# Gated delta-rule attention: scores' mask moved into the decay factors, and four buffers of attention factors

## The reference

```python
def step(S, xs):
    qt, kt, vt, gt, bt = xs
    S = S * jnp.exp(gt)[..., None, None]
    kv = jnp.einsum('bhk,bhkv->bhv', kt, S)
    delta = (vt - kv) * bt[..., None]
    S = S + jnp.einsum('bhk,bhv->bhkv', kt, delta)
    o = jnp.einsum('bhk,bhkv->bhv', qt * scale, S)
    return (S, o)
...
s = _L0_attn_ref(xn, ...)
g = _silu(_L0_ffn_ref(xn, ...))
x = x + s * g
```

## Time and profile before

| what | value |
|---|---|
| device time, median of 3 runs | 4069.94 us (4063.95 to 4076.19) |
| span of the profiled execution | 4068.1 us (its own device time is not given apart from the span) |
| PE busy | 3999.3 us, 98% |
| PEld busy | 3042.7 us, 75% |
| DVE busy | 3147.1 us, 77% |
| ACT busy | 2279.5 us, 56% |
| POOL busy | 1482.6 us, 36% |
| mean granted TensorE clock | 0.995 of full speed |

### The profile page before, as it was taken

How to read it: one execution, slowest core, us unless ns; L and a number is a source line. 1 busy time by engine, 2 the same in 40 slices (tenths; PEclk the granted TensorE clock), 3 DMA queues, 4 the chain that set the end, 5 groups by cost and what they waited for, 6 DMA issues and landing times. The chain is left out here.

```text
span 4068.1 us, 83861 instructions
## 1 busy us (share of the span) xinstructions
PE 3999.3 (98%) x29432; PEld 3042.7 (75%) x29432; DVE 3147.1 (77%) x6660; ACT 2279.5 (56%) x5904; POOL 1482.6 (36%) x1744
## 2 busy tenths in 40 slices
PE   7999999999999999999999999999999999999998
PEld 6788787787777777777777777777777777777775
DVE  6766666665588878888888887788888888877885
ACT  2222222222277676666767666766666676666664
POOL 2322232322133334333333333334444444444445
PEclk9999999999999999999999999999999999999999
DMA  5212111110534344434434454444444444454443
GB/s 151 51 34 49 31 43 49 25 49 21 163 94 105 105 110 103 104 101 102 102 97 108 105 144 128 110 129 120 111 119 116 114 125 125 119 131 125 119 107 97
DMA packets 813539, 400.89 MB, mean 99 GB/s; under 512 B 475584, under 2 KB 738752, under 8 KB 813120
## 3 DMA queue, kind: packets, MB, share of 16 engines
q1 hardware_dynamic: 777024, 340.30, 32.1%
q10 hardware_dynamic: 36096, 55.24, 4.9%
HBM read 242.70 MB, written 152.63 MB: 97 GB/s over the span
## 5 line engine op out<-in xcount | busy, mean ns | idle before, releaser
L1239 PE MATMUL bank<-xtile,wt 128*128 128x259 f32 x4096 | 1073.2, 391 | 5.2 <-PEq L764 2.5
L1239 PEld LDWEIGHTS bank<-xtile,wt 128*128 128x128 f32 x4096 | 736.9, 191 | 148.7 <-issue 59.6
L1631 ACT ACTIVATE xyinv<-bank 128x512 f16<-128x512 f32 x768 | 451.7, 590 | 320.2 <-PE bank L1574 317.2
L1888 PE MATMUL bank<-wot,xnt 128*128 128x512 f32 x1024 | 537.6, 611 | 1.1 <-DVE xnt L1847 0.8
L1243 PE MATMUL bank<-wt,xtile 128*128 128x512 f32 x1024 | 521.1, 607 | 0.0
L1607 DVE TENSOR_TENSOR wlev<-bank,mask 128x256 f16<-128x256 f32 x768 | 316.8, 413 | 149.9 <-PE bank L1574 146.1
L548 PE MATMUL bank<-hb,wt 128*128 128x128 f32 x2816 | 376.4, 277 | 8.4 <-DVE part L588 5.7
L1269 DVE SCALAR_TENSOR_TENSOR vraw<-bank,taps,vraw 128x256 f32<-128x256 f32 x768 | 363.3, 476 | 27.3 <-ACT vraw L1262 13.5
L548 PEld LDWEIGHTS bank<-hb,wt 128*128 128x128 f32 x2816 | 350.2, 194 | 17.5 <-issue 7.2
L611 POOL TENSOR_TENSOR hid<-part 128x256 f32<-128x256 f32 x176 | 139.0, 790 | 474.2 <-ACT part L603 474.2
L1574 PEld LDWEIGHTS bank<-xyinv,lth 128*128 128x128 f16 x3584 | 202.1, 98 | 146.2 <-issue 71.6
(11 more groups left out here) (217 smaller groups left out, 8609.8 us busy)
## 6 DMA issues: line engine op xcount, KB each, us to landing
v_scratch<-vraw SPq DMA_DIRECT2D x64, 512.0 KB, 3.3
vtok<-v_scratch SPq DMA_DIRECT2D x512, 64.0 KB, 2.2
x_scratch<-tq SPq DMA_DIRECT2D x508, 64.0 KB, 1.8
xnt<-x_scratch SPq DMA_DIRECT2D x508, 64.0 KB, 2.5
grows<-row_scratch ACTq DMA_DIRECT2D x126, 256.0 KB, 3.7
k_scratch<-kraw SPq DMA_DIRECT2D x32, 512.0 KB, 2.6
ktok<-k_scratch SPq DMA_DIRECT2D x256, 64.0 KB, 2.5
b_scratch<-kraw SPq DMA_DIRECT2D x256, 64.0 KB, 1.8
```

The costliest lines, as they stand in the source:

```text
L1239: j = pe.matmul(b_p[:, 0:WIN], wt[:, k, c:c + P], xtile[:, par, k, :], **st)
L1631: act.activation(dst, b_inv[p][:].rearrange("p (a h b s) -> p a h b s", a=2, h=HEADS, s=z), ACT.Copy).then_inc(s[f"xy_sb{p}"], 1)
L1888: i = pe.matmul(b_o[:], xnt[:, h], wot[:, h], start=(h == 0), stop=(h == GV - 1))
```

## The change

The multiplication with the masks is gone as a step. The scan now starts from -300, its mask is 1 everywhere but on the diagonal, and the first element of every row of decays is -300. So the running sum left of the diagonal is at most -300, its exponential is 0, and `gam` itself is masked. `dve_lower` and `dve_attend` read the scores where they lie, in PSUM. The factor 64 enters as a logarithm in the bias, so both products carry it, and `act_eps` multiplies by 1/64 in exchange. What `dve_lower` leaves on the diagonal is overwritten with 64 by GpSimd's `affine_select`, in place of the subtraction of a mask. The bank of the scores is free when `lower` and `attend` are both done. `pt` has four buffers in place of three. `SP` waits once for the -300 to be written before it stores the first rows. The planner's tables follow: no `scores` on VectorE, `decay` 1.25 in place of 1.22, `unit` 0.67 in place of 1.16.

```diff
-PIPE = 3
+PIPE = 4
+FAR = 300.0
...
-M_LT, M_LE, M_OFF, M_NEG, M_L0T, M_EVEN = range(6)
-M_PAST = M_EVEN + (LEVELS - 1) // 2
-N_MASK = M_PAST + HEADS
+M_L0T, M_EVEN = range(2)
+M_OFF = M_EVEN + (LEVELS - 1) // 2
+N_MASK = M_OFF + HEADS
...
-    m[:, M_OFF] = 1.0 - np.eye(P)
-    m[:, M_NEG] = -SCALED * np.eye(P)
+    m[:, M_OFF:] = (1.0 - np.eye(P))[:, None, :]
...
-    m[:, M_LT] = SCALED * (r[:, None] < r[None, :])
-    m[:, M_LE] = r[:, None] <= r[None, :]
-    m[:, M_PAST:] = (r[:, None] < r[None, :])[:, None, :]
...
-                link(dve.tensor_scalar(gout[:, u % 2, :, :, G_LNB, :], soft[:, 1].rearrange("p j (g h) -> p j g h", g=GROUPS), -1.0, None, ALU.mult))
+                link(dve.tensor_scalar(gout[:, u % 2, :, :, G_LNB, :], soft[:, 1].rearrange("p j (g h) -> p j g h", g=GROUPS), -1.0, math.log(SCALED), ALU.mult, ALU.add))
...
-            act.activation(grow[:, u % 2], bank[0][0:w, 3 * w:3 * w + P], ACT.Copy).then_inc(s["gc_exp"], 1)
+            act.activation(grow[:, u % 2, 1:P], bank[0][0:w, 3 * w + 1:3 * w + P], ACT.Copy).then_inc(s["gc_exp"], 1)
...
+                    if u == 0:
+                        sp.wait_ge(s["set"], 3)
...
+                pool.memset(grow[:, :, 0:1], -FAR).then_inc(s["set"], 1)
...
-                return [(s["kq_sb"], q + 1)]
+                return [(s["lt_sb"], q + 1), (s["pt_sb"], q + 1)]
...
-        def dve_scores(dve, n):
-            dve.wait_ge(s["kq_ps"], n + 1)
-            if n:
-                dve.wait_ge(s["lt_sb"], n)
-                dve.wait_ge(s["pt_sb"], n)
-            dve.tensor_tensor(kqm[:].rearrange("p (t h) c -> p t h c", t=2), tile_bank("scores", n)[:].rearrange("p (t h c) -> p t h c", t=2, h=KPB),
-                              mask[:, M_LT:M_LE + 1, :].unsqueeze(2).broadcast_to([P, 2, KPB, P]), ALU.mult).then_inc(s["kq_sb"], 1)
...
-            dve.tensor_tensor_scan(gam[:].rearrange("p h c -> p (h c)"), grows[:, n % 2], mask[:, M_PAST:, :].rearrange("p h c -> p (h c)"), 0.0, ALU.add, ALU.mult).then_inc(s["sum_sb"], 1)
+            dve.tensor_tensor_scan(gam[:].rearrange("p h c -> p (h c)"), grows[:, n % 2], mask[:, M_OFF:, :].rearrange("p h c -> p (h c)"), -FAR, ALU.add, ALU.mult).then_inc(s["sum_sb"], 1)
...
-        scored = lambda lo: kqm[:, lo:lo + KPB].unsqueeze(2).broadcast_to([P, KPB, REP, P])
+        scored = lambda n, t: tile_bank("scores", n)[:].rearrange("p (t h c) -> p t h c", t=2, h=KPB)[:, t].unsqueeze(2).broadcast_to([P, KPB, REP, P])
...
-            dve.wait_ge(s["kq_sb"], n + 1)
+            dve.wait_ge(s["kq_ps"], n + 1)
...
-            dve.tensor_tensor(by_key(ltm[:]), by_key(gam[:]), scored(0), ALU.mult).then_inc(s["lt_sb"], 1)
+            dve.tensor_tensor(by_key(ltm[:]), by_key(gam[:]), scored(n, 0), ALU.mult).then_inc(s["lt_sb"], 1)
...
-            dve.tensor_tensor(by_key(pt[:, n % PIPE]), by_key(gam[:]), scored(KPB), ALU.mult).then_inc(s["pt_sb"], 1)
+            dve.tensor_tensor(by_key(pt[:, n % PIPE]), by_key(gam[:]), scored(n, 1), ALU.mult).then_inc(s["pt_sb"], 1)
...
-            pool.tensor_tensor(ltm[:], ltm[:], mask[:, M_NEG, :].unsqueeze(1).broadcast_to([P, HEADS, P]), ALU.subtract).then_inc(s["lti_sb"], 1)
+            pool.affine_select(ltm[:], ltm[:], [[0, HEADS], [1, P]], ALU.not_equal, SCALED, base=0, channel_multiplier=-1).then_inc(s["lti_sb"], 1)
...
-            act.activation(reps[:], split(b_s0), ACT.Copy).then_inc(s["e_sb"], 1)
+            act.activation(reps[:], split(b_s0), ACT.Copy, scale=1.0 / SCALED).then_inc(s["e_sb"], 1)
...
-        lane("dve build", (step for n in units for step in [("dve", "scores", n), ("dve", "decay", n), ("dve", "lower", n), ("dve", "attend", n)]))
+        lane("dve build", (step for n in units for step in [("dve", "decay", n), ("dve", "lower", n), ("dve", "attend", n)]))
...
-                return [("dve", "scores", q)]
+                return [("dve", "lower", q), ("dve", "attend", q)]
...
-                ("dve", "scores"): [("pe", "scores", n)],
...
-                ("dve", "lower"): [("act", "decay", n), ("dve", "scores", n), ("pool", "low", n - 1)],
-                ("dve", "attend"): [("act", "decay", n), ("pe", "answer", n - PIPE)],
+                ("dve", "lower"): [("act", "decay", n), ("pe", "scores", n), ("pool", "low", n - 1)],
+                ("dve", "attend"): [("act", "decay", n), ("pe", "scores", n), ("pe", "answer", n - PIPE)],
```

More of the change, by code:

```diff
@@ L18 @@
+import math
 from contextlib import ExitStack
@@ L89, in constants @@
     c[:, C_ONE] = 1.0
-    m[:, M_LT] = SCALED * (r[:, None] < r[None, :])
-    m[:, M_LE] = r[:, None] <= r[None, :]
-    m[:, M_PAST:] = (r[:, None] < r[None, :])[:, None, :]
-    even = m[:, M_EVEN:M_PAST].reshape(P, LEVELS - 1, P // 2)
+    even = m[:, M_EVEN:M_OFF].reshape(P, LEVELS - 1, P // 2)
     for lv in range(LEVELS):
@@ L1080, in attention @@
         pout, yout = prow, grow
-        kqm, gam = sb("kqm", [P, 2 * KPB, P]), sb("gam", [P, HEADS, P])
+        gam = sb("gam", [P, HEADS, P])
         ltm, pt = sb("ltm", [P, HEADS, P]), sb("pt", [P, PIPE, HEADS, P])
@@ L1110, in attention @@
             "rows_in", "out_ps", "po_sb", "yo_sb", "stored",
-            "kq_ps", "kq_sb", "sum_sb", "gam_sb", "lt_sb", "lti_sb", "lth_sb", "ltl_sb", "pt_sb", "kend_sb",
+            "kq_ps", "sum_sb", "gam_sb", "lt_sb", "lti_sb", "lth_sb", "ltl_sb", "pt_sb", "kend_sb",
             *(f"{n}{p}" for p in range(2) for n in ("y1_sb", "w_ps", "w_sb", "xy_ps", "xy_sb", "er_ps", "c_ps", "c1_sb", "c2_sb", "yf_sb")),
@@ L1566, in even_mask @@
         def even_mask(lv):
-            return mask[:, M_EVEN:M_PAST, :].rearrange("p a c -> p (a c)")[:, (lv - 1) * (P // 2):lv * (P // 2)].rearrange("p (b s) -> p b s", s=1 << lv)
+            return mask[:, M_EVEN:M_OFF, :].rearrange("p a c -> p (a c)")[:, (lv - 1) * (P // 2):lv * (P // 2)].rearrange("p (b s) -> p b s", s=1 << lv)
         def each_head(pe, dst, lhsT, rhs, done=None, start=True, stop=True, cols=P):
@@ L2055, in after @@
             if at == ("dve", "weigh"):
-                return [("sp", "wload", n)] if n else [("dve", "scores", 0)]
+                return [("sp", "wload", n)] if n else [("dve", "attend", 0)]
             if at == ("pool", "knorm"):
@@ L2119, in attention @@
             ("act", "query"): 1.15, ("act", "eps"): 0.61, ("act", "norm"): 1.27,
-            ("dve", "conv"): 0.50, ("dve", "keys"): 1.25, ("dve", "back"): 0.71, ("dve", "queries"): 1.25, ("dve", "scores"): 0.70, ("dve", "decay"): 1.22, ("dve", "lower"): 0.69, ("dve", "attend"): 0.69,
+            ("dve", "conv"): 0.50, ("dve", "keys"): 1.25, ("dve", "back"): 0.71, ("dve", "queries"): 1.25, ("dve", "decay"): 1.25, ("dve", "lower"): 0.69, ("dve", "attend"): 0.69,
             ("dve", "start"): 0.42, ("dve", "level"): 0.42, ("dve", "error"): 1.04, ("dve", "second"): 0.69, ("dve", "third"): 0.69,
@@ L2123, in attention @@
             ("sp", "kstore"): 0.45, ("sp", "qstore"): 0.45, ("sp", "qload"): 3.7, ("sp", "kload"): 3.7, ("sp", "bstore"): 1.85, ("sp", "bload"): 2.6, ("sp", "vstore"): 0.45, ("sp", "vload"): 1.95, ("sp", "xstore"): 1.85, ("sp", "xload"): 2.7, ("sp", "rates"): 0.45, ("sp", "rows"): 1.35, ("sp", "store"): 0.45, ("sp", "wload"): 6.9, ("dve", "weigh"): 0.50,
-            ("pool", "knorm"): 2.30, ("pool", "keys"): 1.22, ("pool", "qnorm"): 0.45, ("pool", "unit"): 1.16, ("pool", "low"): 1.16, ("pool", "kend"): 1.25,
+            ("pool", "knorm"): 2.30, ("pool", "keys"): 1.22, ("pool", "qnorm"): 0.45, ("pool", "unit"): 0.67, ("pool", "low"): 1.16, ("pool", "kend"): 1.25,
             ("pool", "gated"): 1.27, ("pool", "norm"): 2.42, ("pool", "out"): 2.7,
@@ L2252, in _ @@
                         dve_queries(dve, *i)
-                    elif kind == "scores":
-                        dve_scores(dve, *i)
                     elif kind == "decay":
```

## The result

The changed kernel takes 4047.02 us (median of 4 executions, 4045.92 to 4049.74), the kernel before 4066.94 (median of 4, 4063.13 to 4076.19). The ratio is 0.9949, with a 95% interval of 0.9935 to 0.9963: 20 us faster, where the likeliest case had 12 and the range reached down to 4036. The profiled execution took 4047.76 us, its span is 4045.9, so 22.2 us less than the profiled span before.

What follows compares the result with a forecast made beforehand. TensorE was taken to set the pace, so only its waits could be won: -6 behind VectorE, -6 behind ScalarE, -2 at the end, +2 for the held bank, together -12, giving 4058 us; range 4036 to 4086.

Steps and rivals of the forecast that it cites:

- the likeliest case: Whole kernel: a modest gain of 12 us, time 4058 us, own range 4050 to 4064; chance 0.46.
- The masking step goes: VectorE: 128 masking instructions of 684 ns vanish, 87.5 us less work, worth nothing by itself on TensorE's path.
- products from PSUM: VectorE's `lower` and `attend`: 684 ns each without stretching, 27.6 us less in all, bounds 0 to 35.
- keeps its length: VectorE's scan: stays at 1370 ns mean, 175.3 us, and goes on being stretched.
- The select: GpSimd: about 0.85 us, bounds 0.524 and 1.209, no effect on the end; slow-select rival 4066 us, chance 0.04.
- The held bank: Scores' PSUM bank, held until both products finish: 2 us charged; rival 32 us of stalls, 4090 us, chance 0.12.
- (a): TensorE's waits directly behind VectorE: half of the 12 us lost there is won, -6.
- (b): TensorE's waits behind ScalarE: a fifth of 29 us, from operations late because of VectorE, is won, -6.
- the larger gain: Rival, TensorE's waits: nearly all of (a), two thirds of (b), 4 at the end, -35, 4035 us; chance 0.16.
- (c): Towards the end, where TensorE has little filler and VectorE's stretched products lie close to its path: -2 us.
- (d): Scores' PSUM bank held longer, so TensorE may stall: +2 us.
- no-effect rival: Whole kernel: stalls are DMA and chain latency, with as many elsewhere; 4070 us, 4063 to 4077; chance 0.22.

Runs made afterwards that it cites:

- pad, four buffers: Changed kernel plus a planned half-precision VectorE transpose of constants nobody reads, ahead of each scan; 4064.14 us, ratio 0.9983 to the kernel before.
- copy, three buffers: Changed kernel with three buffers; VectorE copies the scores from PSUM to SBUF, both products read the copy, planned; 4066.06 us, ratio 0.9989 to the kernel before.
- pad, three buffers: Changed kernel with three buffers plus a planned VectorE transpose of constants nobody reads, ahead of each scan; 4087.26 us, ratio 1.0043 to the kernel before.
- copy, four buffers: Changed kernel with VectorE copying the scores to SBUF in half precision, both products reading the copy, planned; 4115.53 us, ratio 1.0116 to the kernel before.
- copy, same order: Changed kernel, its instruction order kept, plus an unplanned half-precision copy of the scores directly ahead of each `lower`; 4133.67 us, ratio 1.0166 to the kernel before.

## Why the prediction was right or wrong

**What bounds it.** Right: TensorE sets the pace, and what it loses to waits is all that could be won. The ledger of weight-load waits follows the time over all kernels. For each profiled execution, what is lost behind ScalarE and behind VectorE (rows of 1.2 us or more, less 0.286 us for each wait), and the span:

| kernel | behind ScalarE | behind VectorE | sum | span |
|---|---|---|---|---|
| changed, loads planned 5.2 | 7.7 | 9.9 | 17.6 | 4038.5 |
| changed | 12.1 | 9.1 | 21.2 | 4045.9 |
| select twice | 15.6 | 10.4 | 26.0 | 4045.4 |
| pad, four buffers | 21.1 | 12.2 | 33.3 | 4065.2 |
| changed, scan planned 1.22 | 19.1 | 15.7 | 34.8 | 4065.5 |
| four buffers planned as three | 20.6 | 14.2 | 34.8 | 4073.8 |
| three buffers | 22.7 | 14.4 | 37.1 | 4072.8 |
| before, loads planned 5.2 | 24.5 | 14.0 | 38.5 | 4072.4 |
| before, scan planned 1.25 | 29.7 | 10.5 | 40.2 | 4078.2 |
| before | 29.1 | 12.1 | 41.2 | 4068.1 |
| copy, three buffers | 29.4 | 14.7 | 44.1 | 4070.8 |
| pad, three buffers | 42.0 | 11.9 | 53.9 | 4084.6 |
| copy, four buffers | 40.2 | 29.6 | 69.8 | 4114.6 |
| copy, same order | 34.5 | 49.5 | 84.0 | 4131.0 |

From the first to the last row the sum grows by 66 us and the span by 92; between them the spans stray from that line by up to 11 us. It says where the time is lost, not why an order has it.

**The masking step goes; products from PSUM.** Right in each part: 87.5 us of masking gone, products at 674 and 677 ns and none above 689. VectorE's total fell by 119 for the 115 forecast, which is partly this order's luck (70 with the scan planned at 1.22). The Trainium skill (SBUF — State Buffer, section Who interferes with whom) has a VectorE instruction with two SBUF inputs contend with GpSimd's reads, and one with at most one such input not; the trace after agrees, 689 ns at most against 1764. The kept copies show the way back, 792 and 732 ns. The Trainium skill's higher fixed cost of a PSUM source (VectorE: DVE Perf Modes, the section on the TRN2 errata) does not show in these products: 677 against 682.

**The scan** "keeps its length" was wrong in the mean, 71 ns a unit (9 us of VectorE). In the changed kernel with 1.22 it is at 1396, in the copy with the same order at 1412, so its length is no property of the edit. The traces show what it goes by. Scans that start while no GpSimd instruction runs take 1218 ns at most before (53 of 128) and 1225 at most after (59); the others have means of 1482 (75) and 1379 (69) and a maximum of 2187. The undisturbed scan has kept its length, and fewer and shorter meetings with GpSimd made the mean smaller.

**The select.** 703 ns in the mean, between the two bounds and below the 0.85 taken; hidden, as the doubled one shows by adding nothing.

**The held bank.** Two lines of 1.0 and 0.9 us, for the 2 charged and the 32 of the rival. The reason was the one given: scan and exponential moved ahead of the scores, 4.3 us of holding where 8 were allowed. The version that would show the price, the held bank in the old order, wasn't tried: with the bank given back only by `attend`, that order has no way on, as in the earlier trace rows the convolution of the third next projection stands ahead of `attend` in VectorE's list.

**The sum.** (a) directly behind VectorE: -3 for -6. (b) behind ScalarE: -17 for -6; this is the term that was mis-sized; the larger gain's two thirds of (b), 19, fit better, though its -12 for (a) and -4 for the end do not. (c) the end: 0 for -2. (d) the bank: +1 to +2 for +2. Together about -18 for -12, beside 22.2 of the spans.

**What failed in its reasoning** is that (b) was treated as a fraction of stalls that VectorE's lateness causes, with everything else staying put. That four buffers alone gain at most 1 us is right of the buffer (the kernel planned for three and given four gains nothing) and wrong of the edit, since the number enters the plan: 27 us against the kernel with three, 29 against the one planned for three. The step that moved most, the new lists, had no term in the sum and stood only among the things that would make it wrong. With the same planned numbers on both sides, the changed kernel against the one before is:

| scan, loads planned | before | changed | difference |
|---|---|---|---|
| 1.22, 3.7 | 4068 | 4070 | +2 |
| 1.25, 3.7 | 4079 | 4047 | -32 |
| 1.22 / 1.25, 5.2 | 4073 | 4041 | -33 |

In the first two rows the scan's number is the same on both sides, in the last each kernel has its own. The mean is -21 with a standard deviation of 20, and the pairs lie between the no-effect rival and the larger gain. Counting the order planned for three buffers too, the changed kernel's instructions ran in four orders, 4041, 4047, 4070 and 4076 (mean 4059), those of the kernel before in three, 4068, 4073 and 4079 (mean 4074). The lighter kernel reaches better orders, but so few of them do not set its mean apart. That the forecast had the direction and the range right is thus in part luck: with 1.22 planned for the scan, as before, the same instructions show no gain.

**What is shown, and what stays open.** Shown: work added on VectorE reaches TensorE with 0.78 us for each us in a fixed order, so VectorE's load can cost TensorE time. That taking work away gives it back is argued from this, and the pads' 0.19 to 0.25, where the plan allows for the work, lie within the scatter of orders. Shown too: the order alone moves the time by 10 and 23 us at a change of 0.03 us in one number, as much as the gain. Not settled: how much of these 20 us is relief and how much a fortunate order. 119 us at 0.19 to 0.25 would be 23 to 30, near the measured 20, but that slope comes from the two pads, and the kept copies (-8 and +68) contradict any single slope. Late keys and queries explain a part at best: ScalarE waited for them 40.3 us before, 27.4 after, 66 and 116 us in the kernels with three buffers and with the copy and four, yet 84 in the copy with three buffers, which is as fast as before, and 23.3 in the kernel before with loads of 5.2, which is not faster.

## What to carry to other kernels

Where a planner writes the order and the bounding engine is 98% busy, change one of the plan's numbers in both versions, better several, before an edit gets credit for some 20 us: the scatter over such orders is the error bar, and the interval of the timing is not. Read what the bounding engine loses from the waits of its queue less the ordinary gap, by releaser, since recorded idle time shows a part of it. And since such orders differ by tens of us at no cost in code, trying several numbers of the plan is worth while in itself: the best version came from 5.2 for 3.7 us of load, though the same number made the kernel before no faster.

## What the runs showed of the hardware that was not expected

GpSimd's select over 128x512 has a median of 641 ns, where its subtraction of a mask from the same tile took 1209 in the mean. The two differ in the operation and in the second input; no run told these apart. Beside VectorE's scan, which has two SBUF inputs, one select was stretched to 1.64 us, the maximum of all 128. And the same VectorE product with the same output took 674 to 677 ns with one input in PSUM and 732 to 792 with both in SBUF, so that here an operand left in PSUM was faster in the mean than its copy, before the copy itself is counted. The undisturbed product is the same either way (medians of 676 to 684 with both inputs in single precision); what the mean loses is the instances that meet a GpSimd instruction.
